# Two Swin-style blocks on one core: the second block's small products in column tiles of 32 rows, and its two transpositions placed anew

## The chip, the core and the metric

The kernel runs on one core of a Trainium2 chip. The metric is the device time of one launch in microseconds (us); less is better. The core has a tensor engine (TensorE, PE in the rows; its weight loads are PEld), a vector engine (VectorE, DVE), a scalar engine (ScalarE, ACT), GpSimd (POOL) and a sync engine that issues the transfers (SyncE, SP). Each engine works through its own instructions in order and waits on semaphores for the others.

## What is computed

Two transformer blocks, one after the other, on 32 images of 56 x 56 positions with 96 channels, all in float32. The first is a shifted-window block (windows of 7 x 7, 12 heads); the change doesn't touch it. The second, cut to what matters:

```
def _L1_conv_ref(x, g1, b1, w_qkv, b_qkv, w_proj, b_proj, g2, b2, w_fc1, b_fc1, w_fc2, b_fc2):
    shortcut = x
    xn = layernorm(x, g1, b1)
    windows, Hp, Wp = window_partition(xn, 8)          # 8 x 8 = 64 positions each
    attn_out = attention(windows, w_qkv, b_qkv, w_proj, b_proj)   # 6 heads of 16
    x = shortcut + window_unpartition(attn_out, 8, Hp, Wp, H, W)
    h = layernorm(x, g2, b2)
    h = gelu(einsum('bhwc,cd->bhwd', h, w_fc1) + b_fc1)           # 96 -> 384
    h = einsum('bhwc,cd->bhwd', h, w_fc2) + b_fc2                 # 384 -> 96
    return x + h
```

## The kernel before

`plain_block` computes the second block. Eight windows (four pairs, 512 positions) are a group; there are 196 groups. It is a software pipeline written out by hand: for every engine a function `body(g, phase)` lists that engine's steps of one turn, and a step `name(d, ...)` works on group g + d, so that one turn holds steps of groups g + 3 down to g - 4. `run_groups` writes the first and last turns out and puts the others into a loop of 36 turns per iteration. Nothing else sets the order: each engine takes its steps as `body` lists them.

The steps of TensorE in one turn, in order, are `scores(0)`, `turn_probs(-1, 2)` (three transpositions of exponentials), `keys(1)`, `turn_probs(-1, 3)`, `queries(1)`, `mix(-1)` (exponentials times values, 24 products into three column tiles of 32 output rows, 64 columns moved each), `values(1)`, `turn_x(2)`, `project(-2)`, half of `output(-4)`, `turn_x1(-3)`, the other half of `output(-4)`, and three `hidden(-3, c)` with `turn_probs(0, 0)` and `turn_probs(0, 1)` between them. `turn_x` transposes the normalised input of the block, `turn_x1` that of the MLP; both write the one PSUM bank `psT`, so each waits until the other's content has been read. `output` is fc2, 384 -> 96, and `values`, `project`, `output`, `keys`, `queries` and `hidden` share two PSUM banks, A and B, whose turns `free(...)` guards.

A float32 product appears in the trace as two matmul records, a transposition as one, and `keys`, `queries` and `hidden` are three records of 512 columns each. In `output` a pair's 128 positions are the stationary side and 96 columns are moved; `project` is alike; in `values` 64 positions (half of the array's columns, `odd` choosing which half) are stationary and 48 columns are moved.

ScalarE copies what `turn_x` has made twice (`copy_x`, then `high_x`, the part in reduced precision) and what `turn_x1` has made once (`high_x1`); VectorE makes the low part of the latter (`low_x1`), and `hidden` waits for it. ScalarE also has the exponentials and the GELUs. These need different function tables, so that each turn has two table loads: one ahead of the three `gelu(-3, c)`, with `copy_turned(0, 0)` and `copy_turned(0, 1)` between them, and one behind. `turn_probs(0, 1)` needs the PSUM bank that `copy_turned(0, 0)` empties. GpSimd normalises both inputs (`power_x`, `norm_x`, `power_x1`, `norm_x1`) and scales the exponentials.

Of the kernel before, what the change touches and what calls it, by code (L numbers as in the profile page):

```python
# [40 lines left out]
PAIRS = 4  # L41
# [918 lines left out]
def plain_block(nc, cfg, src, dst, par, const, psum):  # L960
# [14 lines left out]
    with ctx:  # L975
# [174 lines left out]
        with nc.Block() as block:  # L1150
# [48 lines left out]
            def _(pe):  # L1199

                def body(g, phase):
# [59 lines left out]
                    def values(d, bank):  # L1261
                        if exists(g + d, groups):
                            pe.wait_ge(did['xT'], upto(g + d))
                            for w in range(WINDOWS):
                                for odd in range(2):
                                    cols = w_qkv[:, 2 * DIM:3 * DIM].rearrange('c (h o d) -> c h o d', o=2, d=D)[:, :, odd, :]
                                    out = psM[odd * HALF:odd * HALF + WIN, bank, w * HP * D:(w + 1) * HP * D]
                                    last = nc.tensor.matmul(out, xT[:, parity(d), w * WIN:(w + 1) * WIN], cols, start=True, stop=True)  # L1268
                            last.then_inc(did['v_made'], 1)

                    def project(d, bank):
                        if exists(g + d, groups):
                            pe.wait_ge(did['mixedT'], upto(g + d))
                            for p in range(PAIRS):
                                last = nc.tensor.matmul(psM[0:TT, bank, p * DIM:(p + 1) * DIM], mixedT[0:DIM, parity(d), p * TT:(p + 1) * TT], w_proj[0:DIM, :], start=True, stop=True)  # L1275
                            last.then_inc(did['proj_made'], 1)
# [6 lines left out]

                    def output(d, h, bank):
                        if exists(g + d, groups):
                            pe.wait_ge(did['hid'], upto(g + d, CHUNKS - 1, CHUNKS))
                            for p in (2 * h, 2 * h + 1):
                                for c in range(CHUNKS):
                                    last = nc.tensor.matmul(psM[0:TT, bank, p * DIM:(p + 1) * DIM], hid[:, c, p * TT:(p + 1) * TT], w_fc2[:, c, :], start=c == 0, stop=c == CHUNKS - 1)  # L1289
                            if h == 1:  # L1290
                                last.then_inc(did['fc2_made'], 1)

                    def turn_x(d):
                        if exists(g + d, groups):
                            pe.wait_ge(did['x_norm'], upto(g + d))
                            pe.wait_ge(did['x1T_low'], upto(g - 4))
                            pe.wait_ge(did['xT'], upto(g + d - 1))
                            for p in range(PAIRS):
                                last = nc.tensor.transpose(psT[0:DIM, p * TT:(p + 1) * TT], x_norm[:, p, :], ident[0:TT, 0:TT])  # L1299
                            last.then_inc(did['x_turned'], 1)  # L1300

                    def turn_x1(d):
                        if exists(g + d, groups):
                            pe.wait_ge(did['x1_norm'], upto(g + d))
                            pe.wait_ge(did['xT'], upto(g + 2))
                            pe.wait_ge(did['x1T_low'], upto(g + d - 1))
                            for p in range(PAIRS):
                                last = nc.tensor.transpose(psT[0:DIM, p * TT:(p + 1) * TT], x1_norm[:, p, :], ident[0:TT, 0:TT])  # L1308
                            last.then_inc(did['x1_turned'], 1)
# [10 lines left out]
                    values(1, A)  # L1320
                    turn_x(2)
                    free(('q_hat', 1), ('hid', -4, 2, CHUNKS), ('x1', -3))
                    project(-2, B)
                    free(('v_heads', 1), ('k_hat', 1), ('hid', -4, 1, CHUNKS), ('x2', -5))
                    output(-4, 0, A)
                    turn_x1(-3)
                    output(-4, 1, A)
                    free(('x1', -2), ('q_hat', 1), ('hid', -4, 2, CHUNKS))
# [10 lines left out]
            def _(act):  # L1339

                def body(g, phase):
# [60 lines left out]
                    copy_mixed(-1)  # L1402
                    spread_values(1, A)
                    copy_x(2)
                    high_x(2)
                    exponentials(0, 2)
                    exponentials(0, 3)
                    high_x1(-3)
                    act.preload_act_table_set(GELU_SET)
# [9 lines left out]
            def _(dve):  # L1419

                def body(g, phase):
# [101 lines left out]
                    shift(0, 2)  # L1523
                    shift(0, 3)
                    residual(-2, B)
                    total(0, 0)
                    low_x1(-3)
# [10 lines left out]
            def _(pool):  # L1538

                def body(g, phase):  # L1540
# [49 lines left out]
                    def norm_x1(d):  # L1590
                        if exists(g + d, groups):
# [5 lines left out]
                            nc.gpsimd.tensor_tensor(x1_norm[:, :, :], x1_norm[:, :, :], bcast(rstd2[:, :], 2, DIM), ALU.mult).then_inc(did['x1_norm'], 1)  # L1597

                    power_x(2)
                    norm_x(2)  # L1600
                    residual_x(1)
                    power_x1(-3)
                    norm_x1(-3)
                    scale_probs(0, 0)
# [85 lines left out]
```

## Time and profile before

| | before |
|---|---|
| median of 3 runs | 7320.16 us (7315.06 to 7320.9) |
| span of the profiled execution | 7322.4 us |
| second block's groups | 196, a turn of 14.10 us in the steady loop |
| TensorE, VectorE, ScalarE, GpSimd busy in such a turn | 13.38, 12.50, 11.27, 10.81 us |
| mean granted TensorE clock over the span | 0.988 |

The trace gives no time for the profiled execution other than its span, which is 0.03% above the median. The busy share of an engine says how full it is, not who waits for whom; this is read from the timelines of one turn. In a timeline a row is a run of like instructions: its start, its duration until the last of them has ended, and in brackets how long the engine had nothing in it before and what released it. Matmuls are pipelined, so a row's end lies later than the start of the next; the distance from one start to the next is what a step takes of the engine.

### The profile page before, as it was taken

To read this page: it belongs to the slowest core of one execution; us is meant where nothing else is said; L and a number is where in the kernel's file an instruction comes from. 1 tells how busy PE (TensorE), PEld (TensorE's weight loads), DVE (VectorE), ACT (ScalarE), POOL (GpSimd) and SP (SyncE) were. 2 spreads that over 40 slices of the span, in tenths; PEclk is the share of its full clock that TensorE was granted. 3 is DMA by queue.
4 is the path that set the end of the run, shared out by engine and by line. 5 is a ranking of instruction groups with operands and counts; after the bars stand their busy time and mean duration, and the time that the engine had idled before them with its cause. 6 is when DMAs were issued, how large, how long until landed. Compare 5 with 4: busy or idle time off the path is not lost. (4 is left out here: it accounts for less than half of the span.)

```text
span 7322.4 us, 312543 instructions
## 1 busy us (share of the span) xinstructions
PE 7021.7 (96%) x110894; PEld 5453.8 (74%) x110894; DVE 6310.8 (86%) x13114; ACT 6294.8 (86%) x11444; POOL 5480.1 (75%) x6349
## 2 busy tenths in 40 slices
PE   6999999999999999999999995999999999999998
PEld 4777777777777777777777774777777777777777
DVE  5888888888888888888888885888888888888886
ACT  5999999999998999999999995877887877877877
POOL 3777777777777777777777775777777777777776
PEclk9999999999999999999999997999999999999999
DMA  0111111111111111111111111111111111111111
GB/s 21 29 30 30 30 29 30 29 29 30 30 30 29 30 30 29 30 30 30 29 30 30 30 26 27 44 44 44 44 44 44 44 44 43 44 44 44 45 44 36
DMA packets 367610, 252.62 MB, mean 34 GB/s; under 512 B 271816, under 2 KB 347336, under 8 KB 366152
## 3 DMA queue, kind: packets, MB, share of 16 engines
q1 hardware_dynamic: 366154, 233.04, 12.4%
q8 instruction: 934, 15.30, 0.9%
q14 instruction: 522, 4.28, 0.2%
HBM read 78.64 MB, written 77.07 MB: 21 GB/s over the span
## 5 line engine op out<-in xcount | busy, mean ns | idle before, releaser
L879 POOL TENSOR_TENSOR swin_score<-swin_score,swin_top 113x588 f32<-113x588 f32 x1024 | 1203.1, 1175 | 744.2 <-DVE swin_top L751 743.5
L622 ACT ACTIVATE swin_probT<-swin_ps_probs 128x339 f32<-128x339 f32 x2048 | 922.0, 450 | 198.7 <-PE swin_ps_probs L479 177.4
L479 PE MATMUL swin_ps_probs<-swin_ident,swin_prob 113*128 113x113 f32 x6144 | 991.8, 270 | 6.7 <-ACT swin_probT L622 6.7
L1564 POOL TENSOR_TENSOR plain_prob<-plain_prob,plain_inv_total 128x384 f32<-128x384 f32 x784 | 634.4, 830 | 450.1 <-DVE plain_inv_total L1477 450.1
L479 PEld LDWEIGHTS swin_ps_probs<-swin_ident,swin_prob 113*128 113x128 f32 x6144 | 667.9, 141 | 355.1 <-issue 320.7
L746 DVE TENSOR_TENSOR swin_score<-swin_ps_scores,swin_bias_tab 113x588 f32<-113x588 f32 x1024 | 777.9, 760 | 175.1 <-PE swin_ps_scores L469 173.8
L751 DVE TENSOR_REDUCE swin_top<-swin_score 113x12 f32<-113x588 f32 x1024 | 769.0, 751 | 0.2
L628 ACT ACTIVATE swin_prob<-swin_score 113x588 f32<-113x588 f32 x1024 | 719.0, 702 | 5.8 <-POOL swin_score L879 2.9
L782 DVE SCALAR_TENSOR_TENSOR swin_x<-swin_y,swin_y_rstd,swin_x_res 98x96 f32<-98x96 f32 x1024 | 601.7, 645 | 0.8 <-POOL swin_y_rstd L897 0.7
L1289 PE MATMUL plain_ps_dense<-plain_w_fc,plain_hid 128*128 128x96 f32 x4704 | 589.1, 275 | 2.2 <-ACT plain_hid L1362 2.2
L493 PEld LDWEIGHTS swin_ps_mixed<-swin_probT,swin_v_heads 128*32 128x32 f32 x24576 | 422.3, 109 | 222.2 <-issue 145.7
L469 PE MATMUL swin_ps_scores<-swin_k_heads,swin_q_hat 32*64 32x196 f32 (+1 forms) x12288 | 577.8, 347 | 4.6 <-DVE swin_score L746 4.6
L562 PE MATMUL swin_ps_dense<-swin_w_fc,swin_hid 128*98 128x96 f32 x6144 | 577.5, 251 | 1.2 <-ACT swin_hid L699 1.2
L493 PE MATMUL swin_ps_mixed<-swin_probT,swin_v_heads 128*32 128x49 f32 x24576 | 562.8, 210 | 1.7 <-ACT swin_probT L622 1.0
L1289 PEld LDWEIGHTS plain_ps_dense<-plain_w_fc,plain_hid 128*128 128x128 f32 x4704 | 561.4, 193 | 3.2 <-ACT plain_hid L1362 3.0
L562 PEld LDWEIGHTS swin_ps_dense<-swin_w_fc,swin_hid 128*98 128x98 f32 x6144 | 559.6, 168 | 1.5 <-ACT swin_hid L699 1.5
L1362 ACT ACTIVATE plain_hid<-plain_ps_dense,plain_b_fc 128x512 f32<-128x512 f32 x588 | 404.1, 687 | 172.9 <-PE plain_ps_dense L1209 154.9
L1248 PE MATMUL plain_ps_probs<-plain_ident,plain_prob 128*128 128x128 f32 x2352 | 413.6, 285 | 107.5 <-ACT plain_probT L1350 88.8
L1248 PEld LDWEIGHTS plain_ps_probs<-plain_ident,plain_prob 128*128 128x128 f32 x2352 | 263.8, 142 | 327.1 <-issue 298.9
L885 POOL TENSOR_TENSOR swin_x_res<-swin_x_in,swin_res_row 98x384 f32<-98x384 f32 x256 | 256.2, 1001 | 291.2 <-DVE swin_x L782 235.6
L1443 DVE TENSOR_TENSOR plain_score<-plain_ps_scores,plain_top 128x384 f32<-128x384 f32 x784 | 437.2, 558 | 26.8
L1350 ACT ACTIVATE plain_probT<-plain_ps_probs 128x384 f32<-128x384 f32 x784 | 382.4, 488 | 79.3 <-PE plain_ps_probs L1248 71.5
(188 smaller groups left out, 20880.6 us busy)
## 6 DMA issues: line engine op xcount, KB each, us to landing
swin_k_heads<-swin_k_hat SPq DMA_DIRECT2D x1024, 36.8 KB
plain_x_in<-between_blocks SPq DMA_DIRECT2D x784, 48.0 KB, 2.2
plain_k_heads<-plain_k_hat SPq DMA_DIRECT2D x392, 96.0 KB, 2.1
out_dram<-plain_x SPq DMA_DIRECT2D x784, 48.0 KB
swin_x_in<-in_x SPq DMA_DIRECT2D x224, 136.5 KB
between_blocks<-swin_x SPq DMA_DIRECT2D x224, 136.5 KB
swin_x_in<-in_x SPq DMA_DIRECT2D x224, 19.5 KB
between_blocks<-swin_x SPq DMA_DIRECT2D x224, 19.5 KB
```

The source lines that it names most:

```text
L479: last = nc.tensor.transpose(psP[:, n * QT:(n + 1) * QT], prob[0:QT, p, 2 * hp:2 * hp + 2, :].rearrange('p h k -> p (h k)'), ident[0:QT, 0 ...
L493: last = nc.tensor.matmul(psO[32 * band:32 * band + 32, first:first + WIN], v_heads[:, (phase + d) % 4, 2 * p + half, band, n, :], probT[: ...
L562: last = nc.tensor.matmul(psM[0:TT, bank, p * DIM:(p + 1) * DIM], hid[:, c, p * TT:(p + 1) * TT], w_fc2[:, c, :], start=c == 0, stop=c == ...
L622: nc.scalar.activation(to, psP[:, 0:3 * QT], ACT.Copy).then_inc(did['probT'], 1)
L628: nc.scalar.activation(prob[0:QT, p, :, 0:WIN], score[0:QT, p % 2, :].rearrange('p (h k) -> p h k', k=WIN), ACT.Exp).then_inc(did['prob'], 1)
L746: nc.vector.tensor_tensor(score[0:QT, p % 2, :].rearrange('p (b n) -> p b n', b=BANDS), psS[0:QT, :, 0:BC], kind, ALU.add).then_inc(did['s ...
L751: nc.vector.tensor_reduce(top[0:QT, p % 2, :], score[0:QT, p % 2, :].rearrange('p (h k) -> p h k', k=WIN), AX.X, ALU.max).then_inc(did['to ...
L782: last = nc.vector.scalar_tensor_tensor(x1[:, p, :], y[:, p, :], y_rstd[:, p:p + 1], x_res[:, (phase + d) % 4, p, :], ALU.mult, ALU.add)
L879: nc.gpsimd.tensor_tensor(view, view, bcast(top[0:QT, p % 2, :], 2, WIN), ALU.subtract).then_inc(did['shifted'], 1)
L1248: last = nc.tensor.transpose(psP[:, hp * QT:(hp + 1) * QT], prob[0:QT, p, 2 * hp:2 * hp + 2, :].rearrange('p h k -> p (h k)'), ident[0:QT, ...
L1289: last = nc.tensor.matmul(psM[0:TT, bank, p * DIM:(p + 1) * DIM], hid[:, c, p * TT:(p + 1) * TT], w_fc2[:, c, :], start=c == 0, stop=c == ...
L1564: nc.gpsimd.tensor_tensor(pair, pair, bcast(inv_total[0:QT, p // 2, p % 2 * heads:(p % 2 + 1) * heads], 2, WIN), ALU.mult).then_inc(did['p ...
```

## The change

The numbers of rows of one output tile change for three steps of TensorE, the two transpositions trade places, and the other engines' lists follow.

```diff
@@ TensorE, values: 64 rows -> two tiles of 32
-                                    out = psM[odd * HALF:odd * HALF + WIN, bank, w * HP * D:(w + 1) * HP * D]
-                                    last = nc.tensor.matmul(out, xT[:, parity(d), w * WIN:(w + 1) * WIN], cols, start=True, stop=True)
+                                    for part in range(2):
+                                        rows = odd * HALF + 32 * part
+                                        first = w * WIN + 32 * part
+                                        last = nc.tensor.matmul(psM[rows:rows + 32, bank, w * HP * D:(w + 1) * HP * D], xT[:, parity(d), first:first + 32], cols, start=True, stop=True)
@@ project: 128 rows -> four tiles of 32
-                                last = nc.tensor.matmul(psM[0:TT, bank, p * DIM:(p + 1) * DIM], mixedT[0:DIM, parity(d), p * TT:(p + 1) * TT], w_proj[0:DIM, :], start=True, stop=True)
+                                for rows in range(0, TT, 32):
+                                    last = nc.tensor.matmul(psM[rows:rows + 32, bank, p * DIM:(p + 1) * DIM], mixedT[0:DIM, parity(d), p * TT + rows:p * TT + rows + 32], w_proj[0:DIM, :], start=True, stop=True)
@@ output: 128 rows -> four tiles of 32, and in one piece
-                    def output(d, h, bank):
+                    def output(d, bank):
-                            for p in (2 * h, 2 * h + 1):
+                            for p in range(PAIRS):
                                 for c in range(CHUNKS):
-                                    last = nc.tensor.matmul(psM[0:TT, bank, p * DIM:(p + 1) * DIM], hid[:, c, p * TT:(p + 1) * TT], w_fc2[:, c, :], start=c == 0, stop=c == CHUNKS - 1)
-                            if h == 1:
-                                last.then_inc(did['fc2_made'], 1)
+                                    for rows in range(0, TT, 32):
+                                        last = nc.tensor.matmul(psM[rows:rows + 32, bank, p * DIM:(p + 1) * DIM], hid[:, c, p * TT + rows:p * TT + rows + 32], w_fc2[:, c, :], start=c == 0, stop=c == CHUNKS - 1)
+                            last.then_inc(did['fc2_made'], 1)
@@ turn_x, turn_x1: what they wait for
-                            pe.wait_ge(did['x1T_low'], upto(g - 4))
+                            pe.wait_ge(did['x1T_low'], upto(g - 3))
...
-                            pe.wait_ge(did['xT'], upto(g + 2))
+                            pe.wait_ge(did['xT'], upto(g + 1))
@@ TensorE's list
                     values(1, A)
-                    turn_x(2)
+                    turn_x1(-3)
...
                     project(-2, B)
...
-                    output(-4, 0, A)
-                    turn_x1(-3)
-                    output(-4, 1, A)
+                    output(-4, A)
+                    turn_x(2)
...
                     hidden(-3, 0, B)
@@ ScalarE's list
                     spread_values(1, A)
+                    high_x1(-3)
+                    exponentials(0, 2)
+                    exponentials(0, 3)
                     copy_x(2)
                     high_x(2)
-                    exponentials(0, 2)
-                    exponentials(0, 3)
-                    high_x1(-3)
                     act.preload_act_table_set(GELU_SET)
                     gelu(-3, 0, B)
@@ VectorE's list
+                    total(0, 0)
                     residual(-2, B)
-                    total(0, 0)
                     low_x1(-3)
@@ GpSimd's list
+                    power_x1(-3)
+                    norm_x1(-3)
                     power_x(2)
                     norm_x(2)
                     residual_x(1)
-                    power_x1(-3)
-                    norm_x1(-3)
                     scale_probs(0, 0)
```

On TensorE, one turn, from the second half of `queries` and the mix to the first `hidden` (`x1T` is the transposed MLP input, `plain_ps_dense` are banks A and B):

```order
 L1209 MATMUL plain_ps_dense<-plain_xT_high,plain_w_qk_low 96x512
 L1239 MATMUL plain_ps_mixed<-plain_probT,plain_v_heads 32x64 x24
-L1268 MATMUL plain_ps_dense<-plain_w_qkv,plain_xT 64x48 x16
-L1299 MATMUL plain_ps_turn<-plain_ident,plain_x_norm 96x128 x4
-L1275 MATMUL plain_ps_dense<-plain_w_proj,plain_mixedT 128x96 x4
-L1289 MATMUL plain_ps_dense<-plain_w_fc,plain_hid 128x96 x6
-L1308 MATMUL plain_ps_turn<-plain_ident,plain_x_norm 96x128 x4
-L1289 MATMUL plain_ps_dense<-plain_w_fc,plain_hid 128x96 x6
+L1270 MATMUL plain_ps_dense<-plain_w_qkv,plain_xT 32x48 x32
+L1311 MATMUL plain_ps_turn<-plain_ident,plain_x_norm 96x128 x4
+L1278 MATMUL plain_ps_dense<-plain_w_proj,plain_mixedT 32x96 x16
+L1293 MATMUL plain_ps_dense<-plain_w_fc,plain_hid 32x96 x48
+L1302 MATMUL plain_ps_turn<-plain_ident,plain_x_norm 96x128 x4
 L1207 MATMUL plain_ps_dense<-plain_x1T_high,plain_w_fc_high 128x512
```

L1308 is `turn_x1` before and L1311 after, L1299 is `turn_x` before and L1302 after: the MLP input is now turned ahead of `project`, and the block's next input stands last, directly ahead of the first `hidden`, with all of fc2 before it.

On ScalarE before, from the copy of the mix to the second table load:

```order
L1374 ACTIVATE plain_mixedT<-plain_ps_mixed 96x512
L1383 ACTIVATE plain_v_heads<-plain_ps_dense 64x24x16 x2
L1391 ACTIVATE plain_xT<-plain_ps_turn 96x512
L1396 ACTIVATE plain_xT_high<-plain_ps_turn 96x512
L1356 ACTIVATE plain_prob<-plain_score 128x384 x2
L1368 ACTIVATE plain_x1T_high<-plain_ps_turn 96x512
L1409 ACT_TABLE_LOAD
L1362 ACTIVATE plain_hid<-plain_ps_dense,plain_b_fc 128x512
L1350 ACTIVATE plain_probT<-plain_ps_probs 128x384
```

The same piece after:

```order
L1376 ACTIVATE plain_mixedT<-plain_ps_mixed 96x512
L1385 ACTIVATE plain_v_heads<-plain_ps_dense 64x24x16 x2
L1370 ACTIVATE plain_x1T_high<-plain_ps_turn 96x512
L1358 ACTIVATE plain_prob<-plain_score 128x384 x2
L1393 ACTIVATE plain_xT<-plain_ps_turn 96x512
L1398 ACTIVATE plain_xT_high<-plain_ps_turn 96x512
L1411 ACT_TABLE_LOAD
L1364 ACTIVATE plain_hid<-plain_ps_dense,plain_b_fc 128x512
L1352 ACTIVATE plain_probT<-plain_ps_probs 128x384
```

The two copies of the next input now stand directly ahead of the table load and the GELUs; the one copy of the MLP input stood there before.

## Rows read from the trace of the kernel before

**Rows 1.** The page: busy time of each engine, share of the span, instructions.

```profile
PE 7021.7 (96%) x110894; PEld 5453.8 (74%) x110894; DVE 6310.8 (86%) x13114; ACT 6294.8 (86%) x11444; POOL 5480.1 (75%) x6349
```

**Rows 2.** Busy time by stretch (PE, PEld, DVE, ACT, POOL, clock, DMA, GB/s), one group.

```profile
5515.64:5529.74 14.10, 13.38 (x196) 10.82 (x195) 12.50 (x35) 11.27 (x19) 10.81 (x15) 1.00 0.18 44
```

**Rows 3.** Timeline of TensorE in that group: start, duration, instruction, [idle before].

```profile
5515.64 1.12 PE L1227 MATMUL plain_ps_scores<-plain_k_heads,plain_q_hat 32*64 32x128 f32 x48
...
5518.38 0.52 PE L1248 MATMUL plain_ps_probs<-plain_ident,plain_prob 128*128 128x128 f32 x3 [0.46 <-ACT plain_probT L1350]
...
5519.53 1.09 PE L1239 MATMUL plain_ps_mixed<-plain_probT,plain_v_heads 128*32 128x64 f32 x48
5520.55 1.14 PE L1268 MATMUL plain_ps_dense<-plain_w_qkv,plain_xT 128*64 128x48 f32 x32
5521.62 0.64 PE L1299 MATMUL plain_ps_turn<-plain_ident,plain_x_norm 128*96 128x128 f32 x4
5522.10 1.03 PE L1275 MATMUL plain_ps_dense<-plain_w_proj,plain_mixedT 96*128 96x96 f32 x8
5522.97 1.50 PE L1289 MATMUL plain_ps_dense<-plain_w_fc,plain_hid 128*128 128x96 f32 x12
5524.31 0.60 PE L1308 MATMUL plain_ps_turn<-plain_ident,plain_x_norm 128*96 128x128 f32 x4
...
5526.41 0.47 PE L1207 MATMUL plain_ps_dense<-plain_x1T_high,plain_w_fc_high 96*128 96x512 f32 x1 [0.18 <-DVE plain_x1T_low L1448]
...
5528.59 0.52 PE L1248 MATMUL plain_ps_probs<-plain_ident,plain_prob 128*128 128x128 f32 x3
...
5529.74 1.12 PE L1227 MATMUL plain_ps_scores<-plain_k_heads,plain_q_hat 32*64 32x128 f32 x48
```

**Rows 4.** Timeline of ScalarE in the same group.

```profile
5522.74 0.59 ACT L1391 ACTIVATE plain_xT<-plain_ps_turn 96x512 f32<-96x512 f32 x1
5523.24 0.58 ACT L1396 ACTIVATE plain_xT_high<-plain_ps_turn 96x512 fp32r<-96x512 f32 x1
...
5524.94 0.59 ACT L1368 ACTIVATE plain_x1T_high<-plain_ps_turn 96x512 fp32r<-96x512 f32 x1 [0.30 <-PE plain_ps_turn L1308]
5525.56 1.28 ACT L1409 ACT_TABLE_LOAD   x1
5527.38 0.69 ACT L1362 ACTIVATE plain_hid<-plain_ps_dense,plain_b_fc 128x512 f32<-128x512 f32 x1 [0.54 <-PE plain_ps_dense L1209]
5527.97 0.48 ACT L1350 ACTIVATE plain_probT<-plain_ps_probs 128x384 f32<-128x384 f32 x1
```

**Rows 5.** Timeline of VectorE in the same group.

```profile
5519.71 0.74 DVE L1460 TENSOR_SCALAR plain_q_hat<-plain_ps_dense,plain_b_qk 96x512 f32<-96x512 f32 x1
...
5523.17 0.56 DVE L1469 TENSOR_TENSOR plain_x<-plain_ps_dense,plain_x_res 128x384 f32<-128x384 f32 x1 [0.61 <-PE plain_ps_dense L1275]
5523.64 0.94 DVE L1474 TENSOR_REDUCE plain_total<-plain_prob 128x12 f32<-128x768 f32 x1
...
5525.57 0.69 DVE L1448 TENSOR_TENSOR plain_x1T_low<-plain_ps_turn,plain_x1T_high 96x512 fp32r<-96x512 f32 x1 [0.72 <-ACT plain_x1T_high L1368]
```

**Rows 6.** Busy time by stretch, inside the mix of that group.

```profile
5519.70:5519.98 0.28, 0.28 (x24) 0.28 (x21) 0.28 (x2) 0.14 (x1) 0.28 (x1) 1.00 0.00 0
5519.70:5520.26 0.56, 0.56 (x39) 0.56 (x36) 0.56 (x2) 0.14 (x1) 0.56 (x2) 1.00 0.00 0
```

**Rows 7.** Busy time by stretch, late first block and fifth group of the second.

```profile
4377.30:4380.70 3.40, 2.03 (x43) 1.33 (x44) 3.40 (x7) 1.94 (x5) 1.13 (x2) 1.00 0.16 49
4380.70:4384.10 3.40, 3.40 (x21) 3.40 (x22) 1.34 (x3) 1.12 (x3) 3.23 (x4) 0.50 0.01 2
4544.50:4551.30 6.80, 6.12 (x39) 4.61 (x45) 4.86 (x20) 4.00 (x6) 5.30 (x8) 0.50 0.00 1
```

**Rows 8.** Timeline of TensorE in the stretch from 4544.5 us.

```profile
4545.18 0.76 PE L1207 MATMUL plain_ps_dense<-plain_x1T_high,plain_w_fc_high 96*128 96x512 f32 x1 [1.49 <-DVE plain_x1T_low L1448]
...
4550.57 1.47 PE L1227 MATMUL plain_ps_scores<-plain_k_heads,plain_q_hat 32*64 32x128 f32 x48
```

## The prediction

> **What bounds the kernel now.** I began with the busy times [rows 1]: TensorE is at 96%, VectorE and ScalarE at 86%. That tempts one to call the kernel tensor-bound. The busy times of one turn say more [rows 2]: of 14.10 us TensorE is busy 13.38, VectorE 12.50, ScalarE 11.27. So TensorE waits 0.7 us in a turn, and no turn can come below VectorE's 12.5. Then I read the timelines of one turn, taking each time from the start of its scores at 5515.64. TensorE waits twice that is shown [rows 3]: 0.46 us ahead of the transposition at 2.74 (for ScalarE's copy) and 0.18 us ahead of the first hidden chunk at 10.77 (for VectorE's low part). The reader should see two stretches. From 0 to 8.67, where `turn_x1` starts, TensorE leads. From 8.67 to the second transposition of exponentials at 12.95 there is a path over other engines: `turn_x1` starts, ScalarE's copy 0.63 later, the first hidden chunk at 10.77, GELU 0, the copy behind it at 12.33, and 0.62 later the transposition [rows 3, 4]. That path takes 4.28 us, whatever TensorE does meanwhile. Then 1.15 us until the next scores: 8.67 + 4.28 + 1.15 = 14.10.
>
> **Price of the tiles.** Two stretches inside the mix, 0.28 and 0.56 us, touch 24 and 39 records [rows 6]: 15 more in 0.28 us, three column tiles in turn, so a round of three takes 56 ns with 64 columns moved. Each tile is busy with its own record in that time, so I take a fourth tile as free. With 96 columns a round is then 56 x 96/64 = 84 ns, with 48 columns 42 ns. If it did not shrink with columns it would stay 56. Before, fc2 and the projection take 1.34/12 = 112 ns and 0.87/8 = 109 ns a record, the values 1.07/32 = 33 ns [rows 3]. The mix has 16 rounds, 0.90 us, and takes 1.02, so entering and leaving a tiled step costs 0.12.
> - Values: 64 records, 16 rounds of 42 ns, 0.67 + 0.12 = 0.8; with 56 ns 1.02. I take 0.84, against 1.07.
> - Projection: 32 records, 8 rounds of 84 ns, 0.68 (what follows is tiled too), against 0.87.
> - fc2: 96 records, 24 rounds of 84 ns, 2.0 + 0.12 = 2.11, against 1.34 for each of two halves.
>
> The Trainium skill ("TensorEngine Tiling (Array Packing)", Instruction Overhead) says that each matmul has about 60 cycles of overhead and that one should not take the tiling factor from a dimension that is already small. By it, at 2.4 GHz, a record costs at least 25 ns, and the 192 records 4.8 us, an estimate; the mix's 18.7 ns a record [rows 6] disagree with that as a floor.
>
> TensorE's own work thus falls by about 0.7 us of 13.4. The question is whether the turn does.
>
> **Price of the new places.** The steps up to the mix's end at 4.91 don't change. Then values 0.84, `turn_x1` 0.43, projection 0.68, fc2 2.11: `turn_x` could start at 8.97. It also needs the low part of the MLP input, since both use `psT`. `turn_x1` starts at 5.75 and its input is early: GpSimd now makes it first. ScalarE's copy comes after the values' copies, before 7.5. But VectorE is late: the query bias starts when the queries are made, about 4.0; from its start to the end of the two shifts behind it are 2.85 us, then `total` with its reciprocal, now ahead, 1.2, the residual 0.47, and 0.84 from the low part's start to its user [rows 5, 3]. That is 9.1 to 9.3 (ends overlap a little). I take 9.15 as the start of `turn_x`.
>
> Now the path behind it. ScalarE can copy 0.63 later; it copies twice, 0.50 and 0.61; then the table load 1.30; GELU 0 with 0.59 to the next; 0.62 to the transposition: 4.25 us [rows 4, 3]. Before, the table load was hidden: ScalarE ended it at 5526.84, and waited 0.54 for the hidden chunk. Now the load and two copies stand between the transposition and GELU 0. What was taken out of this path (the low part, the first hidden chunk) is as long as what goes in. So the turn is 9.15 + 4.25 + 1.15 = 14.55 us. The reason in one sentence: all of fc2 and the projection now lie ahead of the fixed path of 4.25 us, where half of fc2 lay beside it, and the faster tiles (2.11 + 0.68 + 0.84) don't make up for 1.34 us more in front.
>
> TensorE meanwhile does the transposition (0.48) and two hidden chunks with one transposition (5526.41 to 5528.59, at most 2.18), 2.66 us in a path of 4.25: it stands empty for 1.6 us or more in each turn, in one piece, ahead of `turn_probs(0, 1)`. GpSimd's swap and the residual's wait (x1 is read by the next turn's work) are covered: GpSimd is busy 10.81 of 14.10. The transfers are issued by SyncE with unchanged waits, and are as before.
>
> **The clock.** This gap has a price of its own. In the late first block a stretch of 3.40 us had TensorE busy for 2.03, so 1.37 us empty; in the next 3.40 us its granted clock was 0.50, that is 1.2 instead of 2.4 GHz [rows 7]. In the second block's start-up a gap of 1.49 us ended at 4545.18, and from 4544.5 the clock was 0.50 for 6.8 us [rows 7, 8]. The steady turn with gaps of 0.46 and 0.18 has a clock of 1.00 throughout [rows 2]. A gap of 1.6 us in each turn is on the wrong side of these rows, so I expect the clock to fall in many turns. What it costs: the three hidden chunks with their transpositions take 5.39 us at 0.50 (4545.18 to 4550.57) against 3.33 at 1.00 (5526.41 to 5529.74) [rows 8, 3], a factor of 1.62. A stretch of 3.4 us at that clock loses 1.3 us of TensorE's work, one of 6.8 us loses 2.6; 0.46 us of wait at 2.74 would swallow some. So 0.8 to 2.1 us net, and if it falls in two turns of three 0.5 to 1.4, for which I take 0.85, an estimate.
>
> **Sum.** Per turn +0.45 (order) and +0.85 (clock) = +1.30, over about 192 of 196 groups that run at the full pace: +250 us on the profiled span of 7322, which lies 2 us above the median: 7570.
>
> **Rivals.**
> - *Stall without the clock.* The gap comes, but the clock stays at 1.00, since TensorE is busy otherwise. For it: no row shows a regular pattern of this kind. Then +0.45 x 192 = 86: 7406. Chance 0.26.
> - *Small records have a floor.* If a record can't go below the mix's average of 1.02/48 = 21 ns, the values take 1.36, the projection 0.68, fc2 2.04: `turn_x` at 9.4 to 9.5, +0.3 us more, 7465 with a steady clock and some 7620 without. The page named above points this way, and by its 25 ns the values alone would take 1.6 us. Against it: the rounds' 56 ns are what 64 columns explain. Chance 0.13.
> - *Faster.* The path behind `turn_x` is shorter than I think, and TensorE's saved 0.7 us comes through: 14.10 - 0.70 = 13.4 us a turn, -134 us, 7186. It decides at a start of `turn_x` before 8.67; VectorE's order alone speaks against it (9.1), and would have to be 0.5 us ahead of its own rows. Chance 0.06.
> - *No change.* The start of `turn_x` and path errors cancel, within 0.2% (15 us, about what a measurement of this kernel can tell from no change): 7320. Chance 0.03.
>
> **How the numbers follow.** My forecast, stall and fallen clock, has 0.52. Its own range is +0.45 + 0.4 to +0.45 + 1.6 a turn, 7483 to 7714. The range over the cases reaches down to the steady clock, less 20 us, and up to nearly the forecast's own end: 7385 to 7700. Slower holds in all but the last two cases, 0.91.
>
> **What would show it.** In the changed kernel's trace: fc2 as 96 records in about 2.1 us, the projection 0.7, the values 0.85; TensorE waiting 1.6 us or more ahead of `turn_probs(0, 1)` for ScalarE's `probT`; ScalarE's load of the GELU table directly behind `high_x`, and no wait ahead of GELU 0; a turn of 14.55 us where the clock is 1.00; granted clock clearly below 0.99 in the second block. Wrong would be: no gap there, the table load still hidden, a turn below 14.1, or tiled steps as long as before.

## The result, and the profile after

The changed kernel takes 7780.24 us (median of 4 runs, 7765.97 to 7799.98) against 7320.53 us before: a ratio of 1.0632, 95% interval 1.0615 to 1.0649. It is slower by 460 us, where 250 us was forecast, and above the range.

The page of the changed kernel, busy time and the granted clock in 40 slices (tenths of full speed):

```profile
PE 7137.8 (92%) x135982; PEld 5459.1 (70%) x135982; DVE 6314.5 (81%) x13114; ACT 6289.7 (81%) x11444; POOL 5551.1 (71%) x6349
...
PEclk9999999999999999999999888888888888988888
```

and the clock row of the kernel before:

```profile
PEclk9999999999999999999999997999999999999999
```

Against [rows 1], TensorE has 25,000 more matmuls and hardly more busy time (7138 against 7022 us) in a span that is 451 us longer. In both kernels the clock is at nine tenths or more in the first block. In the second block the kernel before stays there, but for one slice of 7 tenths at the start-up; the changed kernel is at 8 tenths in nearly every slice.

One turn whose clock was 1.00 throughout, on TensorE; it answers to [rows 3]:

```profile
5637.58 1.12 PE L1227 MATMUL plain_ps_scores<-plain_k_heads,plain_q_hat 32*64 32x128 f32 x48
...
5640.32 0.52 PE L1248 MATMUL plain_ps_probs<-plain_ident,plain_prob 128*128 128x128 f32 x3 [0.46 <-ACT plain_probT L1352]
...
5641.47 1.04 PE L1239 MATMUL plain_ps_mixed<-plain_probT,plain_v_heads 128*32 128x64 f32 x45
...
5642.36 0.88 PE L1270 MATMUL plain_ps_dense<-plain_w_qkv,plain_xT 128*32 128x48 f32 x63
5643.17 0.64 PE L1311 MATMUL plain_ps_turn<-plain_ident,plain_x_norm 128*96 128x128 f32 x4
5643.74 0.87 PE L1278 MATMUL plain_ps_dense<-plain_w_proj,plain_mixedT 96*32 96x96 f32 x32
5644.43 2.53 PE L1293 MATMUL plain_ps_dense<-plain_w_fc,plain_hid 128*32 128x96 f32 x96
5646.89 0.64 PE L1302 MATMUL plain_ps_turn<-plain_ident,plain_x_norm 128*96 128x128 f32 x4
...
5651.17 0.52 PE L1248 MATMUL plain_ps_probs<-plain_ident,plain_prob 128*128 128x128 f32 x3 [1.91 <-ACT plain_probT L1352]
...
5652.32 0.44 PE L1227 MATMUL plain_ps_scores<-plain_k_heads,plain_q_hat 32*64 32x128 f32 x9
```

Taken from its scores at 5637.58: the mix at 3.89 as before, `turn_x1` at 5.59 (5.75 forecast: the mix and the tiled values overlap, 1.70 us for both), the projection at 6.16, fc2 at 6.85, `turn_x` at 9.31 (9.15 forecast), the second transposition at 13.59 behind 1.91 us of an empty engine, the next scores at 14.74. From `turn_x` to that transposition is 4.28 us (4.25 forecast). The same turn on ScalarE, answering to [rows 4]:

```profile
5644.81 0.92 ACT L1358 ACTIVATE plain_prob<-plain_score 128x384 f32<-128x384 f32 x2
5647.56 0.59 ACT L1393 ACTIVATE plain_xT<-plain_ps_turn 96x512 f32<-96x512 f32 x1 [1.83 <-PE plain_ps_turn L1302]
5648.06 0.58 ACT L1398 ACTIVATE plain_xT_high<-plain_ps_turn 96x512 fp32r<-96x512 f32 x1
5648.66 1.28 ACT L1411 ACT_TABLE_LOAD   x1
5649.95 0.69 ACT L1364 ACTIVATE plain_hid<-plain_ps_dense,plain_b_fc 128x512 f32<-128x512 f32 x1
5650.54 0.48 ACT L1352 ACTIVATE plain_probT<-plain_ps_probs 128x384 f32<-128x384 f32 x1
```

Copy, copy, table load and GELU 0 follow on each other without a wait; the engine's wait (1.83 us) now lies ahead of the copies. And on VectorE, answering to [rows 5]:

```profile
5641.58 0.75 DVE L1462 TENSOR_SCALAR plain_q_hat<-plain_ps_dense,plain_b_qk 96x512 f32<-96x512 f32 x1
...
5644.35 0.94 DVE L1476 TENSOR_REDUCE plain_total<-plain_prob 128x12 f32<-128x768 f32 x1
...
5645.51 0.56 DVE L1471 TENSOR_TENSOR plain_x<-plain_ps_dense,plain_x_res 128x384 f32<-128x384 f32 x1
5645.98 0.68 DVE L1450 TENSOR_TENSOR plain_x1T_low<-plain_ps_turn,plain_x1T_high 96x512 fp32r<-96x512 f32 x1
```

The low part starts at 8.40 us of the turn and ends at 9.08 (5646.66); with the 0.84 us from its start to its user [rows 5, 3], VectorE allowed `turn_x` at about 9.2 us, as forecast (9.15); it started 0.1 us later, since fc2 took 2.46 us in this turn instead of 2.11, with a pause of 0.26 us between two of its records (the row that merges them does not show it).

Busy time by stretch (PE, PEld, DVE, ACT, POOL, clock, DMA, GB/s), for that turn, for a turn of 17.88 us and for 2000 us of the steady loop:

```profile
5637.58:5652.32 14.74, 12.36 (x325) 9.59 (x324) 11.95 (x34) 11.25 (x19) 11.26 (x15) 1.00 0.15 38
5667.70:5685.58 17.88, 15.65 (x325) 11.97 (x324) 12.60 (x34) 11.27 (x19) 11.54 (x15) 0.79 0.16 39
5000.00:7000.00 2000.00, 1697.39 (x38581) 1314.87 (x38584) 1494.26 (x4061) 1347.34 (x2273) 1338.51 (x1677) 0.87 0.15 38
```

Both turns have 325 matmul records and the other engines' busy times are much alike; TensorE needs 15.65 us for what took it 12.36, and the clock is 0.79. Over the 2000 us it is 0.87, so that at its two levels, 1.00 and 0.50, the engine ran at the lower (1.2 GHz) for 26% of the time; the kernel before has 0.99 over the same stretch.

I also counted in the trace, from one start of the scores to the next, over the 181 turns of the steady loop: 16.66 us on average (14.21 before), 4.41 us of it at the low clock (0.11 before). The 27 turns without any low clock average 14.96 us, the shortest is 14.57. The other 154 hold 5.19 us of low clock each. The wait ahead of the first transposition of exponentials (0.46 us in the turn above, as in [rows 3]) averages 0.46 us in the 27 turns and 0.07 us in the 154.

### The profile page after: what moved, and what is told of

Read it like the earlier page. It is cut to its first block and busy times, and to the rows that moved or that the text cites. A ratio compares the mean times of both kernels' runs of the same rounds, so it can differ in the third digit from the quotient of the medians.

```text
span 7773.8 us, 362732 instructions
## 1 busy us (share of the span) xinstructions
PE 7137.8 (92%) x135982; PEld 5459.1 (70%) x135982; DVE 6314.5 (81%) x13114; ACT 6289.7 (81%) x11444; POOL 5551.1 (71%) x6349
## 3 DMA queue, kind: packets, MB, share of 16 engines
q14 instruction: 522, 4.28, 0.2%
## 5 line engine op out<-in xcount | busy, mean ns | idle before, releaser
L1443 DVE TENSOR_REDUCE plain_top<-plain_ps_scores 128x6 f32<-128x384 f32 x784 | 430.1, 549 | 580.7 <-PE plain_ps_scores L1227 580.7
L1248 PE MATMUL plain_ps_probs<-plain_ident,plain_prob 128*128 128x128 f32 x2352 | 506.4, 335 | 396.7 <-ACT plain_probT L1352 387.6
L1248 PEld LDWEIGHTS plain_ps_probs<-plain_ident,plain_prob 128*128 128x128 f32 x2352 | 336.4, 170 | 630.8 <-POOL plain_prob L1566 426.9
L469 PE MATMUL swin_ps_scores<-swin_k_heads,swin_q_hat 32*49 32x196 f32 (+1 forms) x12288 | 577.3, 347 | 5.2 <-DVE swin_score L746 5.2
L1293 PE MATMUL plain_ps_dense<-plain_w_fc,plain_hid 128*32 128x96 f32 x18816 | 471.4, 248 | 43.4 <-issue 40.3
L1293 PEld LDWEIGHTS plain_ps_dense<-plain_w_fc,plain_hid 128*32 128x32 f32 x18816 | 413.9, 110 | 73.2 <-issue 69.9
```

The costliest lines, as they stand in the source:

```text
L1248: last = nc.tensor.transpose(psP[:, hp * QT:(hp + 1) * QT], prob[0:QT, p, 2 * hp:2 * hp + 2, :].rearrange('p h k -> p (h k)'), ident[0:QT, ...
L1293: last = nc.tensor.matmul(psM[rows:rows + 32, bank, p * DIM:(p + 1) * DIM], hid[:, c, p * TT + rows:p * TT + rows + 32], w_fc2[:, c, :], s ...
```

## The experiments

Ratios are against the kernel before on the same chip, with their 95% intervals. That kernel's medians beside the experiments lie between 7317.24 and 7320.76 us, so differences in us between experiments are good to some 3 us beside their own spread. "The trace" is that of the run in question, and turns are counted as above.

**Tiles or order.** The first kernel has the three tiled steps of the diff in the old order. As a diff to the kernel before:

```diff
@@ values, project and output, nothing else (output is still in two halves)
-                                    last = nc.tensor.matmul(psM[0:TT, bank, p * DIM:(p + 1) * DIM], hid[:, c, p * TT:(p + 1) * TT], w_fc2[:, c, :], start=c == 0, stop=c == CHUNKS - 1)
+                                    for rows in range(0, TT, 32):
+                                        last = nc.tensor.matmul(psM[rows:rows + 32, bank, p * DIM:(p + 1) * DIM], hid[:, c, p * TT + rows:p * TT + rows + 32], w_fc2[:, c, :], start=c == 0, stop=c == CHUNKS - 1)
...
```

> The column tiles of the change alone, with the order, the waits and the lists of the kernel before. If the order is what costs (my theory), there is no gap of 1.9 us ahead of turn_probs(0, 1), the clock stays near 0.98, and a turn is about 13.9 us (the tensor engine reaches turn_x1 by 8.0 us, but GpSimd's normalised MLP input is there only at about 8.5), plus the gaps without a releaser seen in the changed kernel (about 0.35 us a turn): 7250 to 7340 us. If the tiles themselves are what costs (rival: more instructions than the engine is supplied with, and a clock that falls from that), it is well above: 7450 us or more with a clock under 0.97.

Measured: 7334.81 us, 1.0023 (1.0012 to 1.0035). The clock is 0.989 and the large gap is not there, so the order is what costs. But the tiles bring nothing either. What TensorE waits for in 2000 us of its loop (engine, line, releaser: us in total, times, longest):

```profile
PE plain_ps_dense L1207 <- DVE plain_x1T_low L1452: 50.1, 135, 0.6
PE plain_ps_turn L1312 <- POOL plain_x_norm L1601: 24.4, 58, 0.6
...
PE plain_ps_dense L1278 <- issue: 18.3, 33, 1.0
PE plain_ps_dense L1293 <- issue: 16.1, 37, 1.1
```

The saved tensor work went into waits for VectorE's low part (0.18 us a turn before, 0.36 now), for GpSimd's normalised MLP input, and into gaps that have no releaser, "issue".

The second has the order without the tiles:

```diff
@@ the changed kernel, with values, project and output in 64, 128 and 128 rows
-                                    for rows in range(0, TT, 32):
-                                        last = nc.tensor.matmul(psM[rows:rows + 32, bank, p * DIM:(p + 1) * DIM], ...)
+                                    last = nc.tensor.matmul(psM[0:TT, bank, p * DIM:(p + 1) * DIM], ...)
...
```

> The order, the waits and the lists of the change, with values, projection and fc2 as before in 64 and 128 rows. My theory: the input's transposition starts at 4.91 + 1.07 + 0.43 + 0.87 + 2.68 = 9.96 us, the path behind it is 4.25 us and the rest 1.15, so a turn at full clock is 15.4 us, with the same gap of 1.9 us each turn and so a clock that falls for 3 to 5 us of a turn (another 1.2 to 2 us): 7320 + 191 x (1.3 + 1.6) = 7870 us, between 7780 and 7960, clock about 0.94, and no gaps without a releaser in the projection and fc2. Rival (the tiles are to blame for the clock): turn 15.4 us at a steady clock, 7570 us.

Measured: 7873.24 us, 1.0761 (1.0743 to 1.0779), as expected to 3 us; since 1.2 to 2 us a turn were allowed for the clock, hitting it so closely is luck in part. Its loop:

```profile
5000.00:7000.00 2000.00, 1755.17 (x22712) 1429.90 (x22707) 1465.73 (x3973) 1317.44 (x2217) 1301.85 (x1632) 0.86 0.15 37
```

The clock is 0.86 without a single narrow tile among the changed steps. The shortest turn is 15.39 us, the average 17.13, of it 4.73 us at the low clock, and there are no gaps without a releaser, other than the few at the turn of the loop that the kernel before has too. The rival (the tiles pull the clock down) is out.

**Gap or clock.** To part the stall from what the clock makes of it, the gap was filled:

```diff
@@ the changed kernel, TensorE; FILL = 2, in the other run 1
                     hidden(-3, 1, A)
+                    for _ in range(FILL):
+                        nc.tensor.matmul(psO[DIM:128, 0:HIDDEN], w_proj[0:DIM, 0:32], w_fc1[:, :], start=True, stop=True)
                     turn_probs(0, 1)
```

> The changed kernel with two products more ahead of turn_probs(0, 1), of 32 output rows and 384 columns each, written to rows of the mix's PSUM bank that nobody reads; they take about 1.3 us of the gap of 1.9 us in which the tensor engine is empty, and no one waits for them. If the fallen clock is a price of the gap, the clock goes back to about 0.98, a turn to 14.6 us plus 0.35 us of gaps without a releaser, 7320 + 191 x 0.85 = 7480 us. Rival: the clock falls for the narrow tiles or for the gaps without a releaser, or the turn is set by something else: the time stays at 7740 to 7800 us.

> The changed kernel with one product in the gap instead of two, so that about 1.25 us of it stay empty (1.9 in the changed kernel, 0.5 with two). If the clock falls by how long the engine is empty, this lies between: 7517 us if 1.25 us is harmless, 7780 us if it is as bad as 1.9; from the row of before with 1.37 us empty and a clock of 0.50 behind it I expect it to fall in part of the turns, 7530 to 7680 us, mean clock 0.96 to 0.985.

Measured: 7517.46 us with two, 1.0274 (1.0257 to 1.0291), and 7518.36 us with one, 1.0272 (1.0255 to 1.0290). The gap with two, on TensorE:

```profile
5563.74 1.48 PE L1337 MATMUL plain_ps_mixed<-plain_w_fc,plain_w_proj 96*32 96x384 f32 x4
5565.72 0.52 PE L1249 MATMUL plain_ps_probs<-plain_ident,plain_prob 128*128 128x128 f32 x3 [0.50 <-ACT plain_probT L1355]
```

and the loop with two and with one product:

```profile
5000.00:7000.00 2000.00, 1801.16 (x42645) 1298.84 (x42648) 1612.88 (x4431) 1468.89 (x2478) 1455.88 (x1829) 0.99 0.17 42
```

```profile
5000.00:7000.00 2000.00, 1716.49 (x42262) 1268.69 (x42261) 1603.78 (x4429) 1465.20 (x2475) 1452.93 (x1825) 0.99 0.17 42
```

Doing more work made the changed kernel 263 us faster. The transposition still waits for the same copy; the clock is back at 0.99 and the average turn falls from 16.66 to 15.28 us. One product is enough: it leaves 1.14 us empty in a turn, and the low clock falls from 4.41 to 0.21 us a turn. I had expected half an effect, from a stretch of the first block with 1.37 us empty in several pieces [rows 7]. In these runs 1.14 us in one piece is harmless and 1.91 us is not; what lies between wasn't tried.

**The table load.** Copies run under either function table, so the load can go ahead of them, into the wait:

```diff
@@ the changed kernel, ScalarE
+                    act.preload_act_table_set(GELU_SET)
                     copy_x(2)
                     high_x(2)
-                    act.preload_act_table_set(GELU_SET)
                     gelu(-3, 0, B)
```

> The changed kernel with the load of the GELU table ahead of the two copies of the next input, where the scalar engine waits 1.5 us for their transposition. My theory: the path behind turn_x loses the table load (1.30 us), a turn is about 13.3 us at full clock, the gap ahead of turn_probs(0, 1) shrinks from 1.9 to about 0.6 us, and the clock stays up; with 0.35 us a turn for the gaps without a releaser, 7320 - 191 x 0.5 = 7225 us (7170 to 7300). Rival: if the fallen clock comes from the tiles or the supply of instructions, the clock stays near 0.94 and the time above 7400 us.

Measured: 7356.73 us, 1.0049 (1.0032 to 1.0066), clock 0.978. One instruction's place is worth 423 us of the 460. The time is still 130 us over what I expected. TensorE in a turn that began at 5693.13 (the row is the start of the next one), and SyncE's issues in it, show why:

```profile
5708.79 0.47 PE L1227 MATMUL plain_ps_scores<-plain_k_heads,plain_q_hat 32*64 32x128 f32 x12 [2.21 <-DMA plain_k_heads<-plain_k_hat]
```

```profile
5700.91 3.69 SPq L1168 DMA_DIRECT2D plain_x_in<-between_blocks  x4
5704.75 1.24 SPq L1174 DMA_DIRECT2D plain_k_heads<-plain_k_hat  x2
```

The scores waited 2.21 us for the keys' transfer. SyncE issues in order: the input loads first (3.69 us to issue), which wait for `x_res`, and GpSimd now makes that behind both normalisations, at 5700.48. In a turn of 14.6 us this was hidden; in one of 13.2 it isn't. So:

```diff
@@ load-first kernel, GpSimd
+                    residual_x(1)
                     power_x1(-3)
                     norm_x1(-3)
                     power_x(2)
                     norm_x(2)
-                    residual_x(1)
```

> The load-first kernel (the changed kernel, GELU table loaded ahead of copy_x) with GpSimd's residual_x(1) at the head of its list instead of behind both normalisations. In the load-first trace the scores wait up to 2.2 us for the keys' transfer, which SyncE issues behind the input loads, which wait for x_res, made at 6.4 us of a turn. Theory: with x_res at about 1.7 us the keys land before 9 us, the 0.69 us a turn of empty tensor engine ahead of the scores goes, and the rest of the fallen clock with it: turn 13.2 us plus 0.45 us of gaps at instruction fetches, 7360 - 191 x 0.65 = 7235 us (7200 to 7290). Rival: the transfers are late because the DMA engines or the fetches are busy: no change from 7357 us.

Measured: 7259.96 us, 0.9920 (0.9903 to 0.9936). The 0.69 us a turn of empty engine ahead of the scores fell to 0.10, of which most is the turn of the loop. Of the 35 us that remain over the first expectation (7225), some 23 are gaps without a releaser: they take 0.47 us a turn here, where 0.35 was reckoned with.

**The gaps without a releaser.** In the changed kernel, one of them in the projection and one in the transposition behind fc2:

```profile
5610.62 0.88 PE L1270 MATMUL plain_ps_dense<-plain_w_qkv,plain_xT 128*32 128x48 f32 x63
5611.44 0.64 PE L1311 MATMUL plain_ps_turn<-plain_ident,plain_x_norm 128*96 128x128 f32 x4
5612.01 0.35 PE L1278 MATMUL plain_ps_dense<-plain_w_proj,plain_mixedT 96*32 96x96 f32 x2
5613.03 0.78 PE L1278 MATMUL plain_ps_dense<-plain_w_proj,plain_mixedT 96*32 96x96 f32 x27 [0.67 <-issue]
...
5615.80 0.31 PE L1302 MATMUL plain_ps_turn<-plain_ident,plain_x_norm 128*96 128x128 f32 x1
5616.63 0.53 PE L1302 MATMUL plain_ps_turn<-plain_ident,plain_x_norm 128*96 128x128 f32 x3 [0.52 <-issue]
```

and TensorE's waits over the whole second block from 4600 us on:

```profile
PE plain_ps_probs L1248 <- ACT plain_probT L1352: 373.0, 237, 2.1
PE plain_ps_dense L1293 <- issue: 39.2, 92, 1.1
PE plain_ps_scores L1227 <- issue: 18.8, 8, 3.5
PE plain_ps_dense L1278 <- issue: 16.7, 30, 1.2
```

The pages list the transfers of the instruction queue (packets, MB, share), before and after:

```profile
q8 instruction: 934, 15.30, 0.9%
q8 instruction: 1130, 18.51, 1.0%
```

They move 16 KB each. The changed kernel has 196 more of them, one a group, for the 256 instructions more in a turn (128 weight loads and as many matmuls). Counted in the trace there are 1.66 a turn before and 2.65 after. Of the 143 gaps over 0.12 us without a releaser in tiled steps and transpositions of the changed kernel's loop, 95% end 1.2 to 1.6 us after such a transfer has landed; of 104 such gaps in the tiles-only kernel, 96% do. A band of 0.4 us is 6% of the time from one transfer to the next (16.66/2.65 = 6.3 us), so this is no accident. I read it so: TensorE had run through its instructions and stood until the next ones were in. I call these gaps fetch gaps. Three kernels, all built on the residual-first one, are meant to tell number from place:

```diff
@@ which steps have column tiles
  fc2 only:               values 64 rows,  project 128 rows, output 32 rows
  fc2 and projection:     values 64 rows,  project 32 rows,  output 32 rows
  values and projection:  values 32 rows,  project 32 rows,  output 128 rows
```

> The residual-first kernel with column tiles for fc2 only (values in 64 and projection in 128 rows, as before): 144 tensor instructions fewer in a turn than with all tiles, so about 2.1 instead of 2.65 fetches of 256 instructions a turn. The input's transposition can start at 4.91 + 1.07 + 0.43 + 0.87 + 2.11 = 9.39 instead of about 9.15 us, so a turn is 0.25 us longer at full supply, 13.45 us. Theory (gaps come from too many instructions for the fetches): the idle time at fetches falls from about 0.45 to under 0.2 us a turn, and the time is about the same as the residual-first kernel, 7220 to 7280 us. Rival (gaps are a matter of the tile form, not of the number): they stay, 0.3 us or more.

> The residual-first kernel with column tiles for values and projection, fc2 in 128 rows: 112 tensor instructions more in a turn than the kernel before, about 2.1 fetches of 256 instructions a turn (2.65 with all tiles, 2.2 with fc2 only). Theory (number of instructions against the fetches): no gaps in the projection, where the kernels with all tiles had 0.15 us a turn; turn_x at 4.91 + 0.84 + 0.43 + 0.68 + 2.68 = 9.54 less what the vector engine hides, a turn of about 13.7 us, 7215 to 7250 us. Rival (the narrow tiles of 96 input rows in the projection are slow to start by themselves): gaps in the projection as before, 7260 us or more.

(Fc2 tiles only are 112 tensor instructions fewer than all tiles, not 144 as the first of these says.)

> The residual-first kernel with column tiles for fc2 and projection, values in 64 rows: 192 tensor instructions more in a turn than before, about 2.4 fetches a turn, between fc2 only (2.2, no gaps) and all tiles (2.65, 0.45 us of gaps a turn). Turn without gaps 13.36 us (0.19 less than fc2 only). If the gaps start between 2.4 and 2.65: 7200 - 191 x 0.19 = 7165 us. If they are there already: 7190 to 7240 us.

Measured:

| column tiles | us | ratio (95% interval) | fetches a turn | gaps in the loop |
|---|---|---|---|---|
| all (residual-first) | 7259.96 | 0.9920 (0.9903 to 0.9936) | 2.65 | 169, 85 us |
| fc2 only | 7200.51 | 0.9837 (0.9820 to 0.9853) | 2.21 | 0 |
| fc2 and projection | 7179.51 | 0.9808 (0.9792 to 0.9824) | 2.41 | 13, 3 us |
| values and projection | 7294.52 | 0.9968 (0.9956 to 0.9981) | 2.10 | 49, 31 us |

The number of instructions in a turn alone does not order them: 2.41 fetches go nearly without gaps, and 2.10 with values among them have 49. Between the two kernels with tiled values it does: 2.65 fetches have nearly three times the gap time of 2.10. The fc2-only kernel came out 20 us below what I had expected. My expectation for values and projection, no gaps, was wrong; its projection still waits (2000 us of the loop):

```profile
PE plain_ps_dense L1278 <- issue: 13.9, 23, 0.9
```

That kernel's rival, projection tiles that are slow by themselves, doesn't hold either: the kernel with fc2 and projection has the same tiles and 3 us of gaps in all. What the two kernels with many gaps share is the tiled values, the shortest products of all: 64 records with their loads, 128 instructions in 0.82 us, directly behind the mix with its 96; from the start of the mix to `turn_x1` that is 224 instructions in 1.70 us. fc2 takes 192 instructions in 2.1 us and gets them. So I suppose that the rate over a few us is what starves the engine. That it is the rate of just this stretch, and not something else about the values, was not tried by itself.

The turn with fc2 only, at its regular 13.55 us:

```profile
5511.03 1.12 PE L1227 MATMUL plain_ps_scores<-plain_k_heads,plain_q_hat 32*64 32x128 f32 x48
...
5515.95 1.14 PE L1268 MATMUL plain_ps_dense<-plain_w_qkv,plain_xT 128*64 128x48 f32 x32
...
5518.45 2.19 PE L1290 MATMUL plain_ps_dense<-plain_w_fc,plain_hid 128*32 128x96 f32 x96
5520.57 0.64 PE L1299 MATMUL plain_ps_turn<-plain_ident,plain_x_norm 128*96 128x128 f32 x4
...
5523.43 0.52 PE L1248 MATMUL plain_ps_probs<-plain_ident,plain_prob 128*128 128x128 f32 x3 [0.48 <-ACT plain_probT L1349]
...
5524.58 1.12 PE L1227 MATMUL plain_ps_scores<-plain_k_heads,plain_q_hat 32*64 32x128 f32 x48
```

**Two more cuts.** The order and the mended lists without any tiles say what the tiles are worth, and the change with fc2 tiles only says what the fetch gaps cost in it:

> The residual-first kernel without any column tiles: the order of the change, the load ahead of the copies, x_res first, and values, projection and fc2 as before. The input's transposition starts at 9.96 us, the path behind it is 2.95 us and the rest 1.15: 14.06 us a turn, no gaps at fetches, a gap of about 0.6 us ahead of turn_probs(0, 1), clock 0.99: 7310 us (7290 to 7350). It says what the tiles are worth once the order does not hide it: about 75 us against the residual-first kernel, where by tensor work alone it would be 0.7 us a turn, 134 us.

> The changed kernel as it is, with its late table load, but with values and projection in 64 and 128 rows as before. The input's transposition starts 0.25 us later, so a turn without fallen clock is about 14.8 us with no gaps at fetches, against 14.96 on average in the changed kernel (14.57 at best). With the same gap of 1.9 us the clock falls as much, +1.7 us a turn: 16.5 us, 7320 + 191 x 2.35 = 7770 us (7700 to 7830). If it is 7700 or less, the gaps at fetches had a larger part in the fallen clock than I think.

Measured: 7291.86 us, 0.9960 (0.9946 to 0.9975), a turn of 13.96 us; and 7739.55 us, 1.0579 (1.0561 to 1.0596), where the change has 1.0632. Tiles on fc2 and the projection are worth 112 us once the order lets them through, tiles on all three only 32. In the change itself, taking the tiles off values and projection saves 41 us although their tensor work grows: its turns without low clock average 14.97 us, as long as those of the changed kernel, and its low clock is 3.89 us a turn instead of 4.41.

## Why the prediction was wrong

The direction and the mechanism were right. The time missed because one term, the clock, was mis-sized and another, the fetch gaps, was not in the sum. Per turn, 2.45 us measured (16.66 less 14.21) against 1.30:

| term | forecast | measured | from |
|---|---|---|---|
| order: `turn_x` later, fixed path behind it | +0.45 | +0.5 | shortest turns 14.57 to 14.74, 14.10 before |
| gaps at instruction fetches | 0 | +0.35 | turns without low clock, 14.96 less 14.6 |
| clock | +0.85 | +1.7 | 16.66 less 14.96 |

The rows of the table add up to 0.1 us more than 2.45, since they start from the regular turn before, 14.10 us, and the average one, with the ends of the loop's iterations and some low clock, is 14.21.

The filled kernel splits the sum otherwise: with the clock restored the average turn is 15.28 us, so the low clock costs 1.39 us net and everything else 1.07. (The fill is eight instructions a turn and may add to the gaps itself, so 1.39 is the lower bound.) The reason is that the 27 turns are no fair sample: their gaps without a releaser are 0.25 us a turn, those of the other 154 are 0.50 and those of the filled kernel 0.52. The clock's term is therefore 1.4 to 1.7 us where 0.85 was forecast, and the fetch gaps take some 0.35 to 0.45 where nothing was.

- *Price of the tiles.* Right, with the supply there: values 0.82 us (0.84 forecast), projection 0.69 (0.68), fc2 2.12 in the fc2-only kernel (2.11). By the 60 cycles a matmul of the Trainium skill ("TensorEngine Tiling (Array Packing)", Instruction Overhead) the values would take 1.6 us at 2.4 GHz, an estimate; the trace has half of that, 12.8 ns a record. One sum was wrong: by these very prices the tensor work falls by 0.23 + 0.19 + 0.57 = 0.99 us a turn, not 0.7, and it did (busy 13.38 before, 12.36 after). The forecast did not use the 0.7. The rival "faster" did, and should have stood at about 7130 us; so did the 134 us in the expectation for the kernel without tiles, which should have been 190.
- *Price of the new places.* Right: `turn_x` at 9.31 and the path of 4.28 us, both shown by the turn above. `turn_x1` took 0.57 us and not 0.43, which the overlap of mix and values made good. The statement that the table load would lie open was right too; moving it took off 423 us, although 1.3 us a turn are only 250 us. The rest I put down to the clock, 0.978 in that kernel against 0.938.
- *The clock.* That it would fall was right, and shown by the filled gap: 7780 to 7518 us. The step that failed is "if it falls in two turns of three 0.5 to 1.4, for which I take 0.85". It was too small because the clock is low more often and for longer. The 0.85 us stand for 4.5 us of low clock in two turns of three, 3.0 us a turn (1.27 us lost net, 1.73 with the wait of 0.46, at a loss of 0.383 for each us by the factor of 1.62). The trace has low clock in 154 of 181 turns and 5.19 us of it in each, 4.41 us a turn. The loss was too low as well: TensorE's busy time rises from 12.32 us in the turns without low clock to 14.17 on average, 0.42 for each us. That the wait would swallow some was right: 0.46 us in the 27 turns, 0.13 on average.
- *Left out.* "The transfers are issued by SyncE with unchanged waits" was true and too narrow: the instruction stream is a transfer too. The forecast counted TensorE's records for their time and never for their supply, and put the term at nothing.

The rival "small records have a floor" is refuted. "Stall without the clock" is what the filled kernels show, and stood at 7406 us; they take 7518. Gaps without a releaser are 0.52 us a turn in the one with two products, against 0.08 before; the 0.44 more are 84 us of the 112. The other 28 us were not resolved.

## What to carry to other kernels

In a hand-ordered pipeline, ask of each saved microsecond which chain it is taken from, and of each moved step what fixed path hangs behind its new place: here all of fc2 came ahead of a 4.3 us path over ScalarE, and a table load with two copies entered it. A gap of TensorE has two prices, its own length and the clock behind it, and the second can be the larger; filling it with idle products is a quick test of which one is paid. When a step is cut into more and smaller products, count the instructions per microsecond next to the records' time, and try the steps with the wider moving side first. Here fc2 and projection alone, with the load and `x_res` placed early, give 7179.51 us, 1.9% under the kernel before.

## What the runs showed of the hardware

- The granted clock fell without the narrow tiles too (order only, 0.86 in the loop), and with TensorE busy for 1697 of 2000 us in the changed kernel's loop (0.87). With a gap of 1.91 us each turn it fell; with 1.14 us each turn it stayed (0.99).
- Column tiles ran at a sustained 12.8 ns a record (values, 32 output rows, 48 columns). The Trainium skill ("TensorE: Matmul & The Clock Gate", Wait — 56ns, not 53.3ns?) says that starts are never less than about 25 ns apart; the trace disagrees for records in different column tiles.
- TensorE stood still in written-out code without waiting for another engine: gaps of up to 1.2 us in transpositions and tiled products of the changed kernel, 95% of them ending 1.2 to 1.6 us after a 16 KB instruction transfer had landed, in turns where mix and values use 224 instructions in 1.70 us. The kernels without tiled values have 0 to 13 such gaps in the loop, those with them 49 or more.
- A table load took 1.28 us, and the next activation started 1.29 us after its start. The Trainium skill ("ScalarE: Activation LUTs", What ACT_TABLE_LOAD costs) gives 1283 ns, which agrees, and 1380 ns of drain on top, which this trace doesn't show.
